# A fifth chunk of the second MLP matmul in rounded passes instead of fp32

## Chip, core and metric

The kernel runs on one core of a Trainium2 chip. The metric is the device time of one execution in microseconds (us), as the median of several runs. Engines are named as in the profile: PE is TensorE's matmul, PEld its weight load, DVE is VectorE, ACT is ScalarE, POOL is GpSimd, SP issues the transfers.

## What is computed

The input is x, 4 images of 128 channels and 112 x 112 points, fp32. Two blocks follow each other, each as x = x + block(groupnorm(x)). The first is window attention on 8 x 8 windows. The second is linear attention over the whole image with a depthwise convolution and an MLP; the change is in its MLP:

```python
out = out @ Wproj + bproj                                  # after the depthwise convolution
t = _repbn(t + out, bn1_g, bn1_b, bn1_m, bn1_v, alpha1)
ff = jax.nn.gelu(t @ Wfc1 + bfc1, approximate=False) @ Wfc2 + bfc2
t = _repbn(t + ff, bn2_g, bn2_b, bn2_m, bn2_v, alpha2)
```

Wfc1 is 128 x 1024, Wfc2 1024 x 128.

## The kernel before

One image after another goes through three stages, its x staying in SBUF (`ximg`): window attention, the statistics of the linear attention, and a stage over 28 blocks of 4 image rows (448 columns), which does the rest of the second block. The change is in this last stage, here called the MLP stage; it runs 28 steps per image, 112 in all. The program is written by hand, engine by engine, in a fixed order with semaphores, and the loop over blocks is unrolled four steps at a time (`block_loop`).

The hidden width of 1024 is cut in 8 chunks of 128, j = 0 to 7. In step B:

- PE (`step_d`, `fc1`, `fc2`) does the first matmul of chunk j into one of four PSUM banks, and from j = 4 on, behind it, the second matmul of chunk j - 4, added up in bank 6 or 7. Between them stand matmuls for other blocks: q of block B+4 after chunk 1, the projection of block B+1 after chunk 5, and the attention's output of block B+4 after chunk 7. Then come the second matmuls of chunks 4, 5, 6 and 7, and the next step's first matmul of chunk 0.
- ACT (`hidden`) takes each chunk out of PSUM with a GELU, and between chunks does evacuations and roundings for other blocks: qf and qh after chunk 1, tbh after chunk 2, t1h and wb after chunk 5, oring, ub and dwh around the end of the step.
- DVE does the nine taps of the depthwise convolution for block B+2, and around them subtractions (dwl, ql, tbl, t1l), a normalisation (tf), the mix t1 (the row t) after the projection, and the output yb.
- POOL subtracts hl and adds the residual xw for the next block.

A matmul comes in two forms. In fp32 one call gives two weight loads and two matmul records. In rounded form (`split_mm`, L1090 to L1092) both operands are split into a rounded part ("hi", type fp32r) and what is left over ("lo"), and three passes are added: hi x hi, lo weights x hi, hi weights x lo. All first matmuls and the matmuls for other blocks have the rounded form. Of the second matmul's chunks, those in `SPLIT_J`, 0, 2, 3 and 5, have it, and 1, 4, 6 and 7 are fp32.

A chunk in rounded form costs its operand two more operations. ACT writes the GELU to one of two buffers `hf` (L667) and copies it rounded to `hh` (L670); POOL subtracts the two into `hl` (L489), in the order of the chunks. A chunk in fp32 form has only the GELU, into `hw` (L661). Since `hf` has two buffers, the GELU of the k-th split chunk waits until POOL is done with split chunk k - 2. In the second matmul PE waits for `hl` of that chunk:

```python
k = SPLIT_J.index(j)                                       # ACT, hidden(B, j)
if k >= 2:
    act.wait_ge(hl_ready, B * NS + k - 1)
a.activation(hf[:, k % 2, :], bank[j % FC1_BANKS][:, 0:BLOCK], ACT.Gelu, ...)
act.wait_ge(hf_ready, H + 1)
a.activation(hh[:, k, :], hf[:, k % 2, :], ACT.Copy).then_inc(hh_ready, 1)

for k in range(NS):                                        # POOL, step_d
    pool.wait_ge(hh_ready, B * NS + k + 1)
    g.tensor_tensor(hl[:, k, :], hf[:, k % 2, :], hh[:, k, :].bitcast(F32), ALU.subtract)

pe.wait_ge(hl_ready, B * NS + k + 1)                       # PE, fc2(B, bb, j)
m = split_mm(out, [w[:, k, :] for w in w2s], [hh[:, k, :], hl[:, k, :]], ...)
```

At the start of the program ACT rounds the weights of the split chunks (L504) and DVE subtracts (L742).

Of the kernel before, what the change touches and what calls it, by code (L numbers as in the profile page):

```python
# [45 lines left out]
CM = 1024  # L46
NF = CM // P
QUADS_D = BLOCKS // 4
SPLIT_J = (0, 2, 3, 5)
NS = len(SPLIT_J)  # L50
WHOLE_J = tuple(j for j in range(NF) if j not in SPLIT_J)
FC1_BANKS = 4
# [16 lines left out]
def build(nc, x_d, vec_d, fc1b_d, dw_d, wm_d, cm_d, w1_d, w2_d, sel_d, out_d):  # L69
    with ExitStack() as ctx:  # L70
# [428 lines left out]
        def _(act):  # L499
            a = nc.scalar  # L500
            act.wait_ge(consts_loaded, 16 * NCONST)
            a.activation(w1s[0][:], w1f[:], ACT.Copy)
            for k, j in enumerate(SPLIT_J):
                a.activation(w2s[0][:, k, :], w2[:, j, :], ACT.Copy)  # L504
# [85 lines left out]
            with act.Fori(0, NIMG) as i:  # L590
# [64 lines left out]
                def hidden(B, j):  # L655
# [3 lines left out]
                    act.wait_ge(h_mm, H + 1)  # L659
                    if j not in SPLIT_J:  # L660
                        a.activation(hw[:, WHOLE_J.index(j), :], bank[j % FC1_BANKS][:, 0:BLOCK], ACT.Gelu,  # L661
                                     bias=fc1b[:, j:j + 1]).then_inc(hf_ready, 1)
                        return
                    k = SPLIT_J.index(j)
                    if k >= 2:
# [41 lines left out]
        def _(dve):  # L707
# [32 lines left out]
            d.tensor_tensor(w1s[1][:], w1f[:], w1s[0][:].bitcast(F32), ALU.subtract)  # L740
            for k, j in enumerate(SPLIT_J):
                d.tensor_tensor(w2s[1][:, k, :], w2[:, j, :], w2s[0][:, k, :].bitcast(F32), ALU.subtract)  # L742
# [667 lines left out]
```

## Time and profile before

| | us |
|---|---|
| median of 3 runs | 3083.43 (3077.89 to 3096.36) |
| the profiled execution | 3058.93 |
| its span, first to last instruction | 3057.1 |
| busy in it: PE | 2660.9 (87%) |
| PEld | 2194.2 (72%) |
| DVE | 2283.3 (75%) |
| ACT | 2133.7 (70%) |
| POOL | 1310.8 (43%) |

Durations below are from the profiled execution. A timeline row gives start, duration, engine, line, operation, output <- inputs, shapes, how many were merged (x2: two in a row, with the time from the first's start to the last's end), and in brackets the engine's idle time before it and what ended that. Records of PE overlap, since matmuls are pipelined: the distance from one weight load to the next tells what a pass costs.

### The profile page before, as it was taken

How to read it: one execution, taken by the hardware profiler on the slowest of the kernel's cores; microseconds unless marked ns; L12 is line 12 of the kernel's file. 1: busy time of each engine (PE TensorE's matmuls, PEld its weight loads, DVE VectorE, ACT ScalarE, POOL GpSimd, SP SyncE). 2: the span in 40 equal slices, each digit the busy share in tenths (PEclk: the TensorE clock that was granted, in tenths of full speed). 3: DMA queues.
4: the chain of work that ended last, by engine and by line, in shares of the span. 5: the costliest groups of instructions: out<-in, count | busy, mean ns of one | idle time of the engine just before them, and what ended most of it. 6: DMA issues, size and time to landing. Idle time of an engine off the chain costs nothing.

```text
span 3057.1 us, 76969 instructions
## 1 busy us (share of the span) xinstructions
PE 2660.9 (87%) x28146; PEld 2194.2 (72%) x28146; DVE 2283.3 (75%) x5017; ACT 2133.7 (70%) x4040; POOL 1310.8 (43%) x1210
## 2 busy tenths in 40 slices
PE   2888779999688877999958887799996888879999
PEld 2777678888477766888847777688875776768887
DVE  5777578888377757888747775788875777578885
ACT  2666458998466645998836664689984666468897
POOL 2444334555244432554524443345553444425454
PEclk9999889999799988999979998899997999889999
DMA  3000001111000000111100000011110000000000
GB/s 113 1 0 0 1 0 37 39 36 38 22 1 0 0 1 3 37 36 41 41 14 0 0 1 1 4 40 42 36 40 11 0 0 1 1 7 19 21 18 22
DMA packets 25541, 55.50 MB, mean 18 GB/s; under 512 B 3248, under 2 KB 17584, under 8 KB 25392
## 3 DMA queue, kind: packets, MB, share of 16 engines
q1 hardware_dynamic: 25392, 53.57, 5.3%
q8 instruction: 86, 1.41, 0.2%
q14 instruction: 63, 0.52, 0.1%
HBM read 27.87 MB, written 25.69 MB: 18 GB/s over the span
## 4 chain that ended last, share of the span: by engine, by line
PE 55%; issue 20%; POOL 9%; ACT 9%; DVE 4%; DMA 2%; POOLq 0%; SPq 0%; DVEq 0%; ACTq 0%
PE bank L1090 12%; PE bank L1092 11%; PE bank L1091 11%; PE bank L1307 10%; PE bank L1238 5%; POOL xn_lo L422 4%; POOL k L430 3%; PE bank L1246 3%; ACT kx L532 2%; ACT qs L523 2%; ACT kx L530 2%; DMA ximg<-x_in 1%; DVE bank L956 1%; PE bank L1143 1%; POOL hl L489 1%
## 5 line engine op out<-in xcount | busy, mean ns | idle before, releaser
L489 POOL TENSOR_TENSOR hl<-hf,hh 128x448 fp32r<-128x448 f32 x448 | 516.8, 1154 | 642.6 <-ACT hh L670 642.6
L956 DVE SCALAR_TENSOR_TENSOR bank<-oring,dw,bank 128x448 f32<-128x448 f32 x896 | 614.8, 686 | 20.8
L1307 PE MATMUL bank<-hw,w 128*128 128x448 f32 x896 | 390.8, 538 | 0.0
L1090 PE MATMUL bank<-t1h,w_hi 128*128 128x448 f32 x896 | 366.3, 409 | 24.1 <-DVE t1l L973 24.1
L667 ACT ACTIVATE hf<-bank,fc1b 128x448 f32<-128x448 f32 x448 | 282.1, 630 | 127.6 <-PE bank L1092 127.6
L422 POOL TENSOR_TENSOR xn_lo<-xn,xn_hi 128x512 fp32r<-128x512 f32 x112 | 127.2, 1136 | 481.9 <-ACT xn_hi L517 481.9
L1092 PE MATMUL bank<-t1l,w_hi 128*128 128x448 f32 x896 | 329.2, 367 | 0.0
L1091 PE MATMUL bank<-t1h,w_lo 128*128 128x448 f32 x896 | 327.9, 366 | 0.0
L807 DVE TENSOR_REDUCE mx<-bank 128x8 bf16<-128x512 f32 x448 | 248.3, 616 | 103.4 <-PE bank L1124 103.3
L523 ACT ACTIVATE qs<-bank,par 128x512 f32<-128x512 f32 x112 | 71.0, 634 | 329.6 <-PE bank L1092 329.6
L670 ACT ACTIVATE hh<-hf 128x448 fp32r<-128x448 f32 x448 | 259.3, 579 | 14.2
L661 ACT ACTIVATE hw<-bank,fc1b 128x448 f32<-128x448 f32 x448 | 266.4, 618 | 1.6 <-PE bank L1092 1.6
L1155 PE MATMUL bank<-vx,prob 128*64 128x34 f32 x6272 | 204.6, 225 | 46.2 <-ACT vx L538 44.2
L1155 PEld LDWEIGHTS bank<-vx,prob 128*64 128x64 f32 x6272 | 192.0, 138 | 63.1 <-ACT vx L538 52.6
L788 DVE TENSOR_SCALAR xc<-bank,lnmv,lnrs 128x128 f32<-128x128 f32 x392 | 135.2, 404 | 133.9 <-POOL lnrs L416 133.9
L476 POOL TENSOR_TENSOR xw<-wb,ximg 128x448 f32<-128x448 f32 x112 | 166.7, 1488 | 141.1 <-ACT wb L652 129.4
L1090 PEld LDWEIGHTS bank<-t1h,w_hi 128*128 128x128 f32 x896 | 169.7, 189 | 59.3 <-DVE t1l L973 26.5
L546 ACT ACTIVATE prob<-bank 128x512 f32<-128x512 f32 x448 | 205.9, 551 | 5.7 <-PE bank L1143 5.7
L1307 PEld LDWEIGHTS bank<-hw,w 128*128 128x128 f32 x896 | 168.2, 188 | 52.1 <-issue 41.9
L1090 PE MATMUL bank<-hh,w_hi 128*128 128x448 f32 x448 | 203.6, 454 | 2.3
L1143 PE MATMUL bank<-qs,kx 32*128 32x64 f32 x6272 | 197.2, 273 | 0.0
L1091 PEld LDWEIGHTS bank<-t1h,w_lo 128*128 128x128 f32 x896 | 169.5, 189 | 33.6 <-issue 20.8
(158 smaller groups left out, 6907.1 us busy)
## 6 DMA issues: line engine op xcount, KB each, us to landing
ximg<-x_in SPq DMA_DIRECT2D x56, 448.0 KB, 3.5
y_out<-yb SPq DMA_DIRECT2D x112, 224.0 KB, 1.9
wm<-wm_in SPq DMA_DIRECT2D x1, 512.0 KB, 3.4
w1f<-w_in SPq DMA_DIRECT2D x1, 512.0 KB, 5.6
w<-w_in SPq DMA_DIRECT2D x1, 512.0 KB, 6.5
cm<-cm_in SPq DMA_DIRECT2D x1, 320.0 KB, 3.7
sel_f<-sel_in SPq DMA_DIRECT2D x4, 64.0 KB, 6.2
vec<-vec_in SPq DMA_DIRECT2D x1, 11.0 KB, 1.6
```

The costliest lines, as they stand in the source:

```text
L422: g.tensor_tensor(xns[1][:, gg, 0:n], xn[:, gg, 0:n], xns[0][:, gg, 0:n].bitcast(F32), ALU.subtract).then_inc(xnl_ready, 1)
L489: g.tensor_tensor(hl[:, k, :], hf[:, k % 2, :], hh[:, k, :].bitcast(F32), ALU.subtract).then_inc(hl_ready, 1)
L661: a.activation(hw[:, WHOLE_J.index(j), :], bank[j % FC1_BANKS][:, 0:BLOCK], ACT.Gelu, bias=fc1b[:, j:j + 1]).then_inc(hf_ready, 1)
L667: a.activation(hf[:, k % 2, :], bank[j % FC1_BANKS][:, 0:BLOCK], ACT.Gelu, bias=fc1b[:, j:j + 1]).then_inc(hf_ready, 1)
L670: a.activation(hh[:, k, :], hf[:, k % 2, :], ACT.Copy).then_inc(hh_ready, 1)
L807: m = d.tensor_reduce(mx[:, gg, 32 * j:32 * j + 2 * n], bank[j][:, 0:P * n].rearrange("p (e k) -> p e k", k=64), AX.X, ALU.max)
L956: m = d.scalar_tensor_tensor(acc, src, dw[:, k:k + 1], acc, ALU.mult, ALU.add)
L1090: mm(out, w[0], x[0], start=start, stop=False)
L1091: mm(out, w[1], x[0], start=False, stop=False)
L1092: return mm(out, w[0], x[1], start=False, stop=stop)
L1155: m = mm(bank[6 + h][64 * w2:64 * w2 + 64, c:c + VCOLS], prob[:, j, 2 * t + w2, :], vx[:, gg, 2 * t + w2, j, :], start=True, stop=True)
L1307: m = mm(out, w2[:, j, :], hw[:, WHOLE_J.index(j), :], start=first, stop=last)
```

## The change

Chunk 4 joins the split chunks, so that five of the eight have the rounded form:

```diff
-SPLIT_J = (0, 2, 3, 5)
+SPLIT_J = (0, 2, 3, 4, 5)
 NS = len(SPLIT_J)
 WHOLE_J = tuple(j for j in range(NF) if j not in SPLIT_J)
```

All else follows from this tuple. `NS` is 5: `hh`, `hl` and the split second weights get a fifth slot, `hw` loses one, and the counts that engines wait for go by 5 per step. Chunks 4 and 5 are now k = 3 and k = 4, so the GELU of chunk 4 waits for `hl` of chunk 2, and that of chunk 5 for `hl` of chunk 3. POOL has five subtractions between two residuals xw in place of four. At the start there is one weight rounding more on ACT and one subtraction more on DVE.

On PE, at the end of a step, behind the attention's output (qh, ql with ctx):

```order
 L1091 MATMUL bank<-qh,ctx_lo 128x448
 L1092 MATMUL bank<-ql,ctx_hi 128x448
-L1306 REGISTER_ALU
-L1307 MATMUL bank<-hw,w 128x448
+L1302 REGISTER_ALU
+L1090 MATMUL bank<-hh,w_hi 128x448
+L1091 MATMUL bank<-hh,w_lo 128x448
+L1092 MATMUL bank<-hl,w_hi 128x448
 L1302 REGISTER_ALU
 L1090 MATMUL bank<-hh,w_hi 128x448
```

The fp32 matmul of chunk 4 went, and three passes stand in its place, right ahead of the three of chunk 5; the row ahead of each set (L1302) makes the count of `hl` that PE waits for.

On ACT, in the middle of a step, behind the rounding of chunk 3:

```order
 L670 ACTIVATE hh<-hf 128x448
 L659 REGISTER_ALU
-L661 ACTIVATE hw<-bank,fc1b 128x448
+L666 REGISTER_ALU
+L667 ACTIVATE hf<-bank,fc1b 128x448
+L670 ACTIVATE hh<-hf 128x448
 L659 REGISTER_ALU
 L666 REGISTER_ALU
```

The GELU of chunk 4 goes to `hf` instead of `hw`, with a wait for POOL ahead of it (L666) and the rounded copy behind it; chunk 5 follows.

## Rows read from the trace of the kernel before

**Rows 1.** MLP stage, first image, by stretch: busy us of PE, PEld, DVE, ACT, POOL; granted clock; DMA share, GB/s.
```profile
470.00:740.00 270.00, 270.00 (x1180) 221.19 (x1179) 234.67 (x375) 241.72 (x454) 137.39 (x114) 1.00 0.11 38
```

**Rows 2.** Timeline of PE's weight loads at the end of one step.
```profile
518.33 0.39 PEld L1307 LDWEIGHTS bank<-hw,w 128*128 128x128 f32 x2
...
520.26 0.19 PEld L1307 LDWEIGHTS bank<-hw,w 128*128 128x128 f32 x1 [0.19 <-issue]
520.64 0.19 PEld L1307 LDWEIGHTS bank<-hw,w 128*128 128x128 f32 x1 [0.19 <-issue]
...
521.39 0.19 PEld L1091 LDWEIGHTS bank<-t1h,w_lo 128*128 128x128 f32 x1 [0.19 <-issue]
521.60 0.19 PEld L1092 LDWEIGHTS bank<-t1l,w_hi 128*128 128x128 f32 x1
```

**Rows 3.** Timeline of ACT in the same step.
```profile
510.09 0.64 ACT L667 ACTIVATE hf<-bank,fc1b 128x448 f32<-128x448 f32 x1 [1.07 <-PE bank L1092]
...
515.55 0.62 ACT L661 ACTIVATE hw<-bank,fc1b 128x448 f32<-128x448 f32 x1
516.06 0.63 ACT L667 ACTIVATE hf<-bank,fc1b 128x448 f32<-128x448 f32 x1
516.72 0.58 ACT L670 ACTIVATE hh<-hf 128x448 fp32r<-128x448 f32 x1
517.21 0.56 ACT L651 ACTIVATE t1h<-t 128x448 fp32r<-128x448 f32 x1
...
522.20 0.64 ACT L667 ACTIVATE hf<-bank,fc1b 128x448 f32<-128x448 f32 x1 [1.09 <-PE bank L1092]
```

**Rows 4.** Timeline of POOL in the same step.
```profile
514.12 1.14 POOL L489 TENSOR_TENSOR hl<-hf,hh 128x448 fp32r<-128x448 f32 x1 [1.55 <-ACT hh L670]
515.72 1.16 POOL L489 TENSOR_TENSOR hl<-hf,hh 128x448 fp32r<-128x448 f32 x1 [0.46 <-ACT hh L670]
517.38 1.16 POOL L489 TENSOR_TENSOR hl<-hf,hh 128x448 fp32r<-128x448 f32 x1 [0.50 <-ACT hh L670]
518.70 1.52 POOL L476 TENSOR_TENSOR xw<-wb,ximg 128x448 f32<-128x448 f32 x1 [0.16 <-issue]
```

**Rows 5.** Timeline of DVE in the same step.
```profile
515.76 0.68 DVE L968 SCALAR_TENSOR_TENSOR t<-bank,par,ub 128x448 f32<-128x448 f32 x1 [0.69 <-PE bank L1092]
516.36 0.99 DVE L930 TENSOR_TENSOR tbl<-tf,tbh 128x448 fp32r<-128x448 f32 x1
...
518.59 0.62 DVE L973 TENSOR_TENSOR t1l<-t,t1h 128x448 fp32r<-128x448 f32 x1
```

**Rows 6.** The lines of tbl and of xw: duration in ns, min/median/max, all steps.
```profile
L930 DVE TENSOR_TENSOR tbl<-tf,tbh x112: 612/991/1011, 419.9 to 2991.8; 128x448 fp32r<-128x448 f32 x112
...
L476 POOL TENSOR_TENSOR xw<-wb,ximg x112: 1129/1522/1633, 444.6 to 3040.0; 128x448 f32<-128x448 f32 x112
```

**Rows 7.** Timeline of POOL late in the first image.
```profile
734.95 1.16 POOL L489 TENSOR_TENSOR hl<-hf,hh 128x448 fp32r<-128x448 f32 x1 [0.50 <-ACT hh L670]
736.17 1.42 POOL L476 TENSOR_TENSOR xw<-wb,ximg 128x448 f32<-128x448 f32 x1
```

**Rows 8.** Timeline of DVE late in the first image.
```profile
735.72 0.87 DVE L973 TENSOR_TENSOR t1l<-t,t1h 128x448 fp32r<-128x448 f32 x1
```

**Rows 9.** Timeline of PE's weight loads in one of an image's last four steps.
```profile
754.10 0.19 PEld L1090 LDWEIGHTS bank<-hh,w_hi 128*128 128x128 f32 x1 [0.52 <-POOL hl L489]
754.21 0.19 PEld L1091 LDWEIGHTS bank<-hh,w_lo 128*128 128x128 f32 x1
...
759.00 0.39 PEld L1307 LDWEIGHTS bank<-hw,w 128*128 128x128 f32 x2
```

**Rows 10.** Timeline of POOL in that step.
```profile
752.88 1.16 POOL L489 TENSOR_TENSOR hl<-hf,hh 128x448 fp32r<-128x448 f32 x1 [3.62 <-ACT hh L670]
754.54 2.28 POOL L489 TENSOR_TENSOR hl<-hf,hh 128x448 fp32r<-128x448 f32 x2 [0.50 <-ACT hh L670]
```

**Rows 11.** The line of the second weights' rounding on ACT: duration in ns, min/median/max.
```profile
L504 ACT ACTIVATE w_hi<-w x4: 292/292/293, 12.6 to 13.2; 128x128 fp32r<-128x128 f32 x4
```

## The prediction

> **What bounds the kernel now.** I read first the busy time by stretches, to find the stage that the change touches and the engine that fills it. In the MLP stage of the first image TensorE has 270.00 us busy of 270.00 and a granted clock of 1.00 (the 2.4 GHz level), while ACT has 241.72 and POOL 137.39 [rows 1]. Next I read one step of that stage, one 448-column block, from one engine's timeline to the next. ACT starts the GELU of chunk 0 at 510.09 and the same one of the next block at 522.20: a step takes 12.11 us [rows 3]. ACT stands idle 1.09 us before it, and the releaser is a TensorE matmul. So TensorE sets the pace; a step ends when its passes are through.
>
> What a chunk of the second matmul costs TensorE is read from the distance of the weight loads, since matmul records overlap. In the fp32 chunks 6 and 7 two loads stand 0.375 us apart (520.26, 520.64), and an fp32 chunk has two: 0.75 us. Rounded passes have loads 0.20 to 0.21 apart (521.39, 521.60): three passes, 0.61 us [rows 2].
>
> **The change, part by part.** One more chunk, j = 4, goes from one form to the other in all 112 steps.
>
> TensorE: per step one fp32 matmul goes (0.75) and three rounded ones come (0.61): 0.14 us less, 15.7 us in 112 steps, if its operands are there.
>
> ACT: the GELU of chunk 4 now writes hf and a rounding copy hh follows. A copy holds the queue 0.49 us (516.72 to 517.21), a GELU before its copy 0.66 (516.06 to 516.72) [rows 3], where the old GELU took 0.51 (515.55 to 516.06). So ACT carries 0.64 us more per step, and its 1.09 us of idle would hide that.
>
> POOL: a fifth subtraction hl per step, 1.14 to 1.16 us [rows 4]. POOL's total is far from full, but the five do not lie evenly: chunks 2 to 5 are now four subtractions in a row, and TensorE needs the last one soon. hf has only two buffers, so the GELU of chunk 5 must now also wait for the subtraction of chunk 3.
>
> So I follow one step in absolute time. Subtraction 2 ends at 514.12 + 1.14 = 515.26, ahead of GELU 4 at 515.55: no wait. The copy of 4 starts at 515.55 + 0.66 = 516.21 and ends 0.58 later, 516.79. Subtraction 3 ends at 515.72 + 1.16 = 516.88 [rows 4]. GELU 5 is released by that, about 516.94, its copy starts at 517.60 and ends at 518.18. On POOL, subtraction 4 could start at 516.88.
>
> Here VectorE comes in. Its subtraction tbl, also with two operands in SBUF, starts at 516.36 and lasts 0.99 us to 517.35 [rows 5], where its shortest is 0.612 and its median 0.991 [rows 6]: it gets going only when POOL is done at 516.88, and ends 0.47 later. Before the change nothing is ready on POOL just then: subtraction 5 starts at 517.38, when tbl is through. After it, subtraction 4 is at the door at 516.88, behind a VectorE instruction that already waits. The trace has this meeting once per image: t1l asks at 735.72 while POOL's subtraction runs (734.95 to 736.11), ends at 736.59, and POOL's next, xw, put down as starting at 736.17, ends only at 737.59 [rows 7, 8], 1.00 us after VectorE's end. In the ordinary step xw likewise ends at 520.22, 1.01 us after t1l's end at 519.21 [rows 4, 5]. So I price subtraction 4 at tbl's end plus 1.01 and 0.02 for hl being that much longer than xw where nothing holds it (1.129 at the least [rows 6], hl 1.14 to 1.16): 517.35 + 1.03 = 518.38. Subtraction 5 has its copy (518.18) and follows directly; two in a row take 2.28 us [rows 10], so 1.14 each: 519.52.
>
> The Trainium skill, SBUF — State Buffer, section "Who interferes with whom", says that a VectorE instruction with two SBUF inputs contends with a GpSimd instruction that reads SBUF, the second one blocking fully until the first is done. By that rule the sum is the one made here, +36.6 us; without it that of the first rival, +24. Rows 5 to 8 agree with it: tbl and t1l wait, and then POOL does.
>
> TensorE: how soon it goes on after POOL is seen at the end of an image, where it already waits for a subtraction. That ends at 752.88 + 1.16 = 754.04, and the second weight load, which marks the true start of the first pass, follows at 754.21 [rows 9, 10]: 0.17 us. Chunk 4's first pass starts at 518.33 + 0.20 = 518.53 before [rows 2]; subtraction 4 allows 518.55, a stall of 0.02. Chunk 5 is then due at 519.16, but allowed at 519.52 + 0.17 = 519.69: a stall of 0.53. Net per full step: 0.02 + 0.53 - 0.14 = +0.41 us, a step of 12.52. ACT's own delay does not decide: its copy of 5 ends 0.2 us before POOL comes free, and what follows it (t1h, wb, two GELUs, oring, ub, dwh) moves by 517.60 - 516.72 = 0.88 us, within the 1.09 + 0.41 that ACT then has. t1h now runs from 518.09 to 518.65 (it took 0.56 at 517.21 [rows 3]), so t1l finds subtraction 5 at work until 519.52 and ends near 520.0 in place of 519.21; VectorE is idle 35.3 of the 270 us of rows 1, 1.6 us a step, 0.69 of it before its mix [rows 5], so I take nothing for it. If that cover were gone, all 0.8 us would show.
>
> This holds for the 23 steps of an image in which tbl runs. The last five lack it, and the last four also lack q's two evacuations, so POOL's inputs come earlier. In one of the last four (its chunk 0 is subtracted from 752.88) subtractions 2 and 3 run from 754.54 to 756.82 [rows 10], so GELU 4 is released at 755.76, GELU 5 at 756.9, and the same reckoning gives subtraction 5 an end of 759.36, so 759.53 on TensorE, against 759.00 + 0.20 + 0.61 = 759.81 when chunk 5 is due [rows 9]: no stall, -0.14. I take that for four of the five. In the very last step the projection for a next block is missing, TensorE comes 0.61 earlier and stalls 0.33: +0.19. Per image 23 x 0.41 - 4 x 0.14 + 0.19 = 9.06; four images +36.2.
>
> Setup: one more rounding of a 128x128 weight on ACT, 0.29 us [rows 11], and one subtraction of the same size on VectorE, taken as equal; both lie ahead of TensorE's start, bounds 0 and 0.6, taken +0.4. The longer program costs nothing in my sum: the loop is already unrolled four times, and TensorE is full in it [rows 1].
>
> Sum: +36.6 us on the profiled execution of 3058.93, 3095.5, which is +1.2%. The median of the runs shown, 3083.43, is 0.8% above that execution; the same share gives 3083.4 + 36.9 = 3120.
>
> **The rivals.**
> VectorE and POOL do not hold each other up here. Then subtraction 4 runs 516.88 to 518.03, subtraction 5 starts when its copy is done (518.18 + 0.07) and ends 519.40; TensorE goes on at 519.57, a stall of 0.43, net +0.29 per full step, +24 us, 3107. For it: tbl might get through differently when POOL has work queued. Against it: rows 7 and 8.
>
> The gain stays. Subtraction 5 would have to be done by 519.14 - 0.17 = 518.97, 0.55 earlier than I reckon; ACT and POOL would have to drop behind less than their queues show. Then -15.7 us, 3068, not slower. For it: both engines have idle time in total [rows 1]. Against it: the old subtraction 5 ended at 517.38 + 1.16 = 518.54, only 0.6 us ahead of that point, and one more in front costs 1.1.
>
> A second meeting. If t1l is ready before subtraction 5 starts, VectorE takes its turn in between, 0.48 us more per full step: 92 x 0.48 = 44 on top, 3164. It decides from the point where subtraction 4 ends after 518.7, when t1h is done; I reckon 518.38, so it needs 0.3 us of further delay on POOL.
>
> **How the numbers follow.** Forecast 0.62, engines not holding each other up 0.20, gain stays 0.10, second meeting 0.08. A measurement of this kernel tells about 1% from no change. The forecast, +1.2%, lies just over that: about four fifths of its chance counts as slower (0.49), with the second meeting (0.08) and a little of the first rival (0.03) 0.60; the rest of the forecast (0.13), the first rival (0.17) and most of the gain (0.07) make 0.37 within 1%; 0.03 is left for faster. The range reaches down past the first rival, with the spread of the runs, to 3092, and up to 3150, between forecast and second meeting.
>
> **What would show it.** In the changed profile I expect: steps of about 12.5 us in place of 12.11; a wait of TensorE's weight load for hl of some 0.5 us once per full step, near nothing before; subtraction 4 with a record near 1.5 us; the wait of GELU 5 for POOL, 0.2 to 0.3 us; ACT's idle before GELU 0 at about 0.5. Steps near 11.97 and no wait for hl would make the prediction wrong, as would a subtraction 4 of 1.16 us beside a tbl of 0.99.

## The result and the profile after

| | before | after |
|---|---|---|
| median of 20 runs, us | 3075.82 (3060.12 to 3096.36) | 3098.98 (3089.57 to 3106.16) |
| ratio after / before | | 1.0071, 95% interval 1.0053 to 1.0089 |
| the profiled execution, us | 3058.93 | 3101.64 |
| MLP stage, first to last yb of an image, us | 323.3 in all four | 330.7 in all four |
| a full step of it, us | 12.11 | 12.47 |

The ratio is an estimate with its interval; the quotient of the two medians is 1.0075. The kernel became slower, by less than forecast: 3098.98 us where 3120 was said, +0.7% where +1.2% was said. A second comparison, with the same two kernels (e8 below), gave 1.0087 (1.0063 to 1.0111).

The stage first. TensorE, full before [rows 1], is idle 5 of 270 us; ACT and POOL have more to do; the granted clock is 1.00 again. Since records of PE overlap, this idle time shows only part of what TensorE loses, 0.23 us a step where the passes come 0.50 late, as the weight loads below tell.

```profile
470.00:740.00 270.00, 264.81 (x1170) 215.92 (x1169) 244.20 (x365) 249.63 (x465) 162.13 (x130) 1.00 0.11 38
```

What TensorE waits for is in the view of the waits of the same stretch (total us, times, longest). The second and the last row shown stand in no such view of the kernel before: in 22 steps the first weight load of a split chunk waits 0.6 us for hl, and its matmul up to 0.2.

```profile
ACT hf L667 <- PE bank L1092: 14.1, 22, 0.7
PEld bank L1090 <- POOL hl L489: 13.4, 22, 0.6
...
PE bank L1090 <- POOL hl L489: 5.2, 22, 0.2
```

One full step, engine by engine. ACT (answers to [rows 3]): GELU 0 at 524.86 and 537.34, 12.48 us apart; the copy of chunk 4 at 530.97; then GELU 5 does not follow 0.49 later, at 531.46, but at 531.68, when subtraction 3 is done:

```profile
524.86 0.63 ACT L667 ACTIVATE hf<-bank,fc1b 128x448 f32<-128x448 f32 x1 [0.70 <-PE bank L1092]
...
530.97 0.58 ACT L670 ACTIVATE hh<-hf 128x448 fp32r<-128x448 f32 x1
531.68 0.64 ACT L667 ACTIVATE hf<-bank,fc1b 128x448 f32<-128x448 f32 x1
532.35 0.58 ACT L670 ACTIVATE hh<-hf 128x448 fp32r<-128x448 f32 x1
...
537.34 0.63 ACT L667 ACTIVATE hf<-bank,fc1b 128x448 f32<-128x448 f32 x1 [0.69 <-PE bank L1092]
```

POOL (answers to [rows 4]): subtractions 3, 4 and 5 now run without a gap and are merged in one row. They take 3.77 us, where three at 1.155 would take 3.46: the middle one is stretched to about 1.46.

```profile
528.89 1.15 POOL L489 TENSOR_TENSOR hl<-hf,hh 128x448 fp32r<-128x448 f32 x1 [1.55 <-ACT hh L670]
530.49 3.77 POOL L489 TENSOR_TENSOR hl<-hf,hh 128x448 fp32r<-128x448 f32 x3 [0.45 <-ACT hh L670]
534.33 1.42 POOL L476 TENSOR_TENSOR xw<-wb,ximg 128x448 f32<-128x448 f32 x1
```

VectorE (answers to [rows 5]): tbl waits for subtraction 3 and ends at 532.12, and t1l, 0.62 us before, now takes 1.31, since it meets subtraction 5:

```profile
531.14 0.98 DVE L930 TENSOR_TENSOR tbl<-tf,tbh 128x448 fp32r<-128x448 f32 x1
...
533.43 1.31 DVE L973 TENSOR_TENSOR t1l<-t,t1h 128x448 fp32r<-128x448 f32 x1
```

TensorE's weight loads (answers to [rows 2]): chunk 4's second load is at 533.31; chunk 5's would be due 0.61 later at 533.92 and is at 534.42, 0.16 behind POOL's end at 534.26:

```profile
533.20 0.19 PEld L1090 LDWEIGHTS bank<-hh,w_hi 128*128 128x128 f32 x1
533.31 0.19 PEld L1091 LDWEIGHTS bank<-hh,w_lo 128*128 128x128 f32 x1
533.51 0.19 PEld L1092 LDWEIGHTS bank<-hl,w_hi 128*128 128x128 f32 x1
534.31 0.19 PEld L1090 LDWEIGHTS bank<-hh,w_hi 128*128 128x128 f32 x1 [0.61 <-POOL hl L489]
534.42 0.19 PEld L1091 LDWEIGHTS bank<-hh,w_lo 128*128 128x128 f32 x1
```

### The profile page after: what moved, and what is told of

Same layout as the page of the kernel before. It is cut to its first block, busy times and chain, and to the rows that moved or that the text cites. A ratio compares the mean times of both kernels' runs of the same rounds, so it can differ in the third digit from the quotient of the medians.

```text
span 3099.8 us, 77643 instructions
## 1 busy us (share of the span) xinstructions
PE 2692.7 (87%) x28258; PEld 2219.9 (72%) x28258; DVE 2355.4 (76%) x5018; ACT 2204.0 (71%) x4153; POOL 1457.6 (47%) x1322
## 4 chain that ended last, share of the span: by engine, by line
issue 36%; POOL 32%; PE 17%; ACT 8%; DVE 4%; DMA 2%; POOLq 1%; SPq 0%; DVEq 0%; ACTq 0%
POOL hl L489 20%; PE bank L1238 5%; POOL xw L476 4%; POOL xn_lo L422 4%; POOL k L430 3%; PE bank L1090 3%; PE bank L1246 3%; ACT kx L532 2%; ACT kx L530 2%; ACT qs L523 2%; PE bank L1092 2%; PE bank L1091 2%; DMA ximg<-x_in 1%; PE bank L1143 1%; DVE bank L956 1%
## 5 line engine op out<-in xcount | busy, mean ns | idle before, releaser
L489 POOL TENSOR_TENSOR hl<-hf,hh 128x448 fp32r<-128x448 f32 x560 | 672.4, 1212 | 542.8 <-ACT hh L670 542.8
L667 ACT ACTIVATE hf<-bank,fc1b 128x448 f32<-128x448 f32 x560 | 351.9, 628 | 94.9 <-PE bank L1092 79.8
L670 ACT ACTIVATE hh<-hf 128x448 fp32r<-128x448 f32 x560 | 324.3, 579 | 17.8
L1307 PE MATMUL bank<-hw,w 128*128 128x448 f32 x672 | 288.6, 538 | 0.0
L1090 PE MATMUL bank<-hh,w_hi 128*128 128x448 f32 x560 | 216.4, 386 | 22.9 <-POOL hl L489 20.7
L476 POOL TENSOR_TENSOR xw<-wb,ximg 128x448 f32<-128x448 f32 x112 | 160.2, 1431 | 126.3 <-ACT wb L652 121.2
L1091 PE MATMUL bank<-hh,w_lo 128*128 128x448 f32 x560 | 205.0, 366 | 0.0
L1092 PE MATMUL bank<-hl,w_hi 128*128 128x448 f32 x560 | 202.9, 362 | 0.0
L661 ACT ACTIVATE hw<-bank,fc1b 128x448 f32<-128x448 f32 x336 | 196.5, 617 | 0.0
```

The source lines that it names most:

```text
L476: g.tensor_tensor(xw[:, bb, :], wb[:, bb, :], ximg[:, bass.ds(b * BLOCK, BLOCK)], ALU.add).then_inc(xw_ready, 1)
L1090: mm(out, w[0], x[0], start=start, stop=False)
L1091: mm(out, w[1], x[0], start=False, stop=False)
L1092: return mm(out, w[0], x[1], start=False, stop=stop)
L1307: m = mm(out, w2[:, j, :], hw[:, WHOLE_J.index(j), :], start=first, stop=last)
```

## The experiments

Steps and stages below are worked out from the starts of yb (L982): a stage is the first to the last yb of an image, a full step the mean from the third to the 23rd. Each execution comes with its mean granted clock, so kernels can also be compared at equal clock: a straight line with one slope for all kernels through the 124 executions with a recorded clock gives 1.8 us for each 0.001 and leaves 1.9 us of scatter. In the last column the kernel before itself differs by 2.0 us between the executions beside e1 to e4 (3070.1) and those beside e5 to e8 (3072.0), so differences of that size say nothing there.

| | change | full step | MLP stage | ratio to before (95%) | at a clock of 0.950 |
|---|---|---|---|---|---|
| before | | 12.11 | 323.3 | | 3071.0 (54 runs) |
| after | | 12.47 | 330.7 | 1.0071 (1.0053 to 1.0089) | 3098.6 (20) |
| e1 | before, unaltered | 12.11 | 323.2 | 0.9996 (0.9975 to 1.0018) | in the first row |
| e2 | after, tbl late | 12.39 | 328.8 | 1.0072 (1.0047 to 1.0097) | 3088.4 (4) |
| e3 | after, third hf | 12.49 | 330.8 | 1.0092 (1.0066 to 1.0119) | 3098.6 (4) |
| e4 | after, both | 12.13 | 322.9 | 0.9950 (0.9928 to 0.9972) | 3063.8 (6) |
| e5 | after, late wait for hl | 12.18 | 322.7 | 0.9965 (0.9947 to 0.9984) | 3066.3 (12) |
| e6 | after, all three | 11.97 | 317.7 | 0.9929 (0.9904 to 0.9953) | 3045.7 (6) |
| e7 | before, late wait for hl | 12.11 | 321.6 | 0.9981 (0.9961 to 1.0002) | 3063.5 (12) |
| e8 | after, unaltered | 12.48 | 330.9 | 1.0087 (1.0063 to 1.0111) | 3099.9 (6) |

**e1, the kernel before once more.** No edit.

> The kernel before, unaltered, to see how its own executions spread and what clock each had. Theory of the clock: the executions differ outside the MLP stage, in window attention, by the granted clock; the times of this kernel fall along one line against the clock (about 1.4 us for each 0.001, read from the 20 executions of the changed kernel), and at a clock of 0.956 they lie near 3059, some 30 us under the changed kernel at the same clock; the median lies near 3076 because the usual clock is lower than the 0.956 of the profiled execution. MLP stage from the first to the last yb of an image: 323.3 us in every image, granted clock 1.00. Rival: TensorE, full in the MLP stage, is slowed there in most executions, and the changed kernel hides part of that in its stalls; then the profile shows MLP stages over 324 us or a granted clock under 1.00 in them.

Measured: MLP stages of 323.2 in all four images, where the first trace has 323.3; the rival (TensorE slowed there) falls. The executions of the kernel before, this one's and those beside it, run from 3065.76 us at a clock of 0.953 to 3090.61 at 0.939. So the profiled execution of 3058.93 at 0.956 that the prediction started from was one of the quickest, and what spreads the runs lies outside the MLP stage. By the line above they follow the clock at 1.8 us for each 0.001, not 1.4. The window attention of single images in the two first traces, from its first xg (L766) to its last, shows it. The kernel before, third image, 265 us at a clock of 0.96:

```profile
1560.27:1825.44 265.17, 223.71 (x4402) 180.98 (x4406) 199.71 (x624) 167.43 (x321) 110.95 (x126) 0.96 0.00 0
```

and the kernel after, third and fourth image, 0.92 for 273 us and 0.97 for 265, with the same number of PE's instructions:

```profile
1577.48:1850.15 272.67, 233.53 (x4402) 189.35 (x4406) 199.76 (x624) 167.29 (x321) 110.67 (x126) 0.92 0.00 0
2349.94:2614.95 265.01, 223.14 (x4402) 180.58 (x4406) 199.85 (x624) 167.20 (x321) 110.67 (x126) 0.97 0.00 0
```

Each is a mixture of the two levels, 1.2 and 2.4 GHz (0.50 and 1.00), and the low one lies at its beginning: in the kernel before the first 24 us have 0.58 and the rest 1.00, in the kernel after the first 40 us have 0.56:

```profile
1560.00:1584.00 24.00, 12.88 (x119) 9.83 (x123) 11.12 (x41) 7.66 (x14) 7.24 (x10) 0.58 0.00 1
1584.00:1825.00 241.00, 210.39 (x4286) 170.96 (x4283) 188.15 (x581) 159.76 (x308) 103.60 (x117) 1.00 0.00 0
```

```profile
1577.00:1617.00 40.00, 28.83 (x327) 23.94 (x328) 20.02 (x68) 13.59 (x24) 11.61 (x15) 0.56 0.00 1
```

The statistics stage varies likewise, in e1 from 150.5 us at 0.86 to 156.7 at 0.80. Long and short ones stand in traces of both kernels: in e1, the kernel before, window attention takes 264.7 us in one image and 273.4 in another. Of the 42.7 us between the two profiled executions, 16.8 are of this kind (window attention and statistics of all four images, from the first xg to the first yb: 1683.6 us against 1666.8).

**e2, tbl at the end of the step.**

```diff
-                    if near(5):
-                        tb_low(B + 5, (u + 1) % 2)
                     if near(2):
                         taps(B + 2, (u + 2) % 4, 5, 7, not near(3))
...
                         taps(B + 2, (u + 2) % 4, 7, NTAP, not near(3))
+                    if near(5):
+                        tb_low(B + 5, (u + 1) % 2)
```

> The changed kernel with VectorE's tbl moved from the middle of the step to its end, away from POOL's four subtractions. Theory A (POOL's queue, with the turn that tbl takes in it): subtraction 4 has a record of 1.15 us and ends 0.35 us earlier, but subtraction 5 then waits for its copy (the GELU of chunk 5 still waits for subtraction 3), so it ends only 0.10 earlier, 9.30 us after GELU 0 in place of 9.40: a step of 12.38 us in place of 12.48, MLP stage 328.5 per image in place of 330.7, 9 us less in all. Rival B (tbl and POOL do not hold each other up): no change, 12.48. Rival C (the fp32 matmul's going is not worth 0.14 and the stall is not POOL's): no change.

Measured: 12.39 and 328.8. Subtractions 3 and 4 take 2.29 us together, no longer stretched, and subtraction 5 starts only 0.24 us after them, for want of its copy:

```profile
530.45 1.15 POOL L489 TENSOR_TENSOR hl<-hf,hh 128x448 fp32r<-128x448 f32 x1 [1.55 <-ACT hh L670]
532.05 2.29 POOL L489 TENSOR_TENSOR hl<-hf,hh 128x448 fp32r<-128x448 f32 x2 [0.45 <-ACT hh L670]
534.57 1.15 POOL L489 TENSOR_TENSOR hl<-hf,hh 128x448 fp32r<-128x448 f32 x1 [0.24 <-ACT hh L670]
```

So the turn that tbl takes is real, and what it costs alone is 0.09 us a step, because the copy of chunk 5 is right behind as the next limit. The plain ratio did not move; its four runs had a mean clock of 0.9455. At equal clock it is 10 us below the kernel after, where 7.8 were due from the stages.

**e3, a third hf buffer.**

```diff
-        hf = sb("hf", [P, 2, BLOCK])
+        hf = sb("hf", [P, 3, BLOCK])
...
-                    if k >= 2:
-                        act.wait_ge(hl_ready, B * NS + k - 1)
-                    a.activation(hf[:, k % 2, :], ...)
+                    if k >= 3:
+                        act.wait_ge(hl_ready, B * NS + k - 2)
+                    a.activation(hf[:, k % 3, :], ...)
```

The copy and POOL's subtraction take the same slot, k % 3.

> The changed kernel with a third hf buffer, so that the GELU of chunk 5 waits for subtraction 2 instead of 3. Theory A: the wait of that GELU for POOL (0.23 us) goes, but subtraction 5 still stands behind subtraction 4 in POOL's queue; step 12.48 us, MLP stage 330.7 per image, no change within 1 us. Rival D (the two hf buffers are what delays chunk 5): 0.25 us less per full step, 12.23, some 23 us less in all.

Measured: 12.49 and 330.8, no change; subtractions 3 to 5 take the same 3.77 us:

```profile
528.15 3.77 POOL L489 TENSOR_TENSOR hl<-hf,hh 128x448 fp32r<-128x448 f32 x3 [0.46 <-ACT hh L670]
```

Rival D falls: ACT's wait for the buffer does not decide here. That it is a second limit, 0.2 us below the first, shows in the next run.

**e4, both.** The edits of e2 and e3 together.

> The changed kernel with both: tbl at the end of the step and a third hf buffer. Theory A: subtraction 4 ends at 7.92 us after GELU 0 and subtraction 5, its copy done at 7.84, at 9.07; TensorE's stall falls from 0.53 to 0.2 us; step 12.15 us in place of 12.48, MLP stage near 323 per image, 30 us less in all, which is the kernel before within 0.2%. Rival D: no more than the third buffer alone gives, 12.23. Rival B: what the third buffer alone gives.

Measured: 12.13 and 322.9. The three subtractions take 3.42 us, and TensorE's wait falls from 0.6 to 0.3:

```profile
533.42 3.42 POOL L489 TENSOR_TENSOR hl<-hf,hh 128x448 fp32r<-128x448 f32 x3 [0.45 <-ACT hh L670]
```

```profile
PEld bank L1090 <- POOL hl L489: 6.0, 22, 0.3
```

Neither edit alone was worth more than 0.09 us a step, both are worth 0.34. That is what two limits in a row look like, the POOL queue and, 0.1 to 0.2 us below it, the copy.

**e5, the wait for hl ahead of the third pass only.**

```diff
-                        pe.wait_ge(hl_ready, B * NS + k + 1)
-                        m = split_mm(out, [w[:, k, :] for w in w2s], [hh[:, k, :], hl[:, k, :]],
-                                     start=first, stop=last)
+                        pe.wait_ge(hh_ready, B * NS + k + 1)
+                        mm(out, w2s[0][:, k, :], hh[:, k, :], start=first, stop=False)
+                        mm(out, w2s[1][:, k, :], hh[:, k, :], start=False, stop=False)
+                        pe.wait_ge(hl_ready, B * NS + k + 1)
+                        m = mm(out, w2s[0][:, k, :], hl[:, k, :], start=False, stop=last)
```

> The changed kernel, but TensorE waits for the subtraction hl only ahead of the third pass of a split chunk, the one that reads it; the first two passes wait for the copy hh. Theory A (TensorE's stall is for subtraction 5, whose copy is long done): the third pass of chunk 5 is due 0.41 us after the first, so the stall of 0.53 us per full step falls to about 0.1; step 12.08 us in place of 12.48. In the last four steps of an image the stall of 0.42 at chunk 0, which the kernel before has too, also goes. MLP stage near 320.5 us per image (330.7 changed, 323.3 before). Against the kernel before at equal clock some 11 us less. Rival D (ACT's late copy of chunk 5 is what TensorE waits for): the stall stays, 12.4.

Measured: 12.18 and 322.7, so 0.29 of the 0.40 us came back; 0.10 a step did not. The waits of the weight loads name two causes, hl at the third pass and, new, ACT's GELU of chunk 6, which comes behind the later GELU 5 and the added copy (L1309 is the fp32 matmul, L1306 the third pass):

```profile
PEld bank L1309 <- ACT hw L661: 4.9, 22, 0.2
PEld bank L1306 <- POOL hl L489: 4.8, 22, 0.2
```

A weight load can wait 0.2 us without a loss: e6 below, where TensorE is full, has a row like the first of these. What each costs TensorE shows in the matmul records of one step beside those of e6. The third pass of chunk 5 takes 0.47 us in place of 0.36, and the four fp32 records of chunks 6 and 7 take 1.77 in place of 1.67, about 0.1 us each. The latter in e5 and in e6:

```profile
534.18 1.77 PE L1309 MATMUL bank<-hw,w 128*128 128x448 f32 x4
```

```profile
519.32 1.67 PE L1309 MATMUL bank<-hw,w 128*128 128x448 f32 x4
```

Theory A stands for the stall, about 0.1 us as said, but not for what is next: I had taken ACT's idle time as cover and had not worked out when GELU 6 is due once TensorE comes earlier. Rival D falls: chunk 5's first pass now follows without a wait.

**e6, all three.** The edits of e2, e3 and e5.

> All three: tbl at the end of the step, a third hf buffer, and the wait for hl ahead of the third pass alone. Theory A: subtraction 5 ends 9.07 us after GELU 0 and the third pass is due at 9.46, so no stall is left and the whole 0.14 us of the fifth chunk shows: step 11.97 us, MLP stage near 317.8 per image, against the kernel before some 22 us less at equal clock (0.7% faster), of which 6 to 7 come from the stall at chunk 0 in the last four steps of an image. Rival (another engine, ACT or VectorE, takes over once TensorE no longer waits for POOL): step 12.05 or more.

Measured: 11.97 and 317.7, and 0.9929 of the kernel before: faster than both. TensorE is full again, and the rival falls:

```profile
470.00:740.00 270.00, 270.00 (x1219) 227.68 (x1219) 248.29 (x380) 256.58 (x484) 159.35 (x137) 1.00 0.12 39
```

The weight loads of the third passes of chunks 4 and 5 stand 0.60 us apart, without a wait for POOL:

```profile
518.31 0.19 PEld L1306 LDWEIGHTS bank<-hl,w_hi 128*128 128x128 f32 x1
...
518.91 0.19 PEld L1306 LDWEIGHTS bank<-hl,w_hi 128*128 128x128 f32 x1
```

**e7, the kernel before with the late wait.** The edit of e5 on the kernel before.

> The kernel before with the wait for hl ahead of the third pass alone, to tell how much of the run with all three is not the fifth chunk's. Theory A: full steps stay at 12.11 us, since nothing stalls there; the last four steps of an image lose 0.42 us each: MLP stage 321.6 per image in place of 323.3, 6.7 us less in all. Rival: the late wait itself shortens full steps: under 12.05.

Measured: full steps 12.11, stage 321.6, as said. It parts the gain of e6: the stages of e6 are 317.72 - 321.63 = -3.91 us per image against this one, -15.6 in four (27 of 28 steps in each), which is the 15.7 that the change promised on TensorE (112 x 0.14).

**e8, the kernel after once more.** No edit.

> The changed kernel, unaltered, once more beside the kernel before on this chip. Theory of the clock: MLP stage 330.7 per image again, and at equal clock some 29 us above the kernel before; the plain ratio may differ from that by what the mean clocks differ (0.0039 higher here in the first comparison, worth 7 us). If the clock difference was chance, the plain ratio is 1.009 to 1.010; if it belongs to the kernel, 1.007 again.

Measured: stage 330.9, ratio 1.0087, between the two expectations, with an interval that holds 1.007 as well as 1.010. The medians lie 29.7 us apart here, 23.2 in the first comparison. The mean clock was 0.9485 here and 0.9495 for the kernel before beside it, so here the kernel after had the lower one; in the first comparison it had 0.950, but for the kernel before beside it none is on record. At equal clock the kernel after lies 27.6 us (the 20 executions of the first comparison) and 28.9 us (the six here) above the 54 of the kernel before, 0.9%.

## Why the prediction was right and wrong

The direction and the mechanism were right, the size was not.

- That TensorE fills the stage and that an fp32 chunk costs it 0.75 us and a rounded one 0.61: right. e6 against e7 shows the difference, 15.6 us of 15.7.
- That the fifth subtraction reaches TensorE too late: right. Subtraction 5 was put at 9.43 us after GELU 0 and came at 9.40 (534.26 - 524.86); the stall was put at 0.53 and is 0.50.
- That tbl takes a turn between subtractions 3 and 4: right. The second of three is stretched to 1.46 us, and e2 removes that. The first rival, without the turn, falls. By e2 the turn is worth 0.09 us a step, where the forecast and this rival lie 0.12 apart.
- That ACT's own delay does not decide: right by e3, though by little, as e4 shows. That it is covered was right only as long as TensorE stalls; e5 shows GELU 6 as the next wait. ACT's idle before GELU 0 is 0.69 us, where about 0.5 was expected.
- t1l's delay at no cost: the step lengths agree. Its end came at 534.74, 9.88 after GELU 0, where 9.9 was said.
- The second meeting (t1l between subtractions 4 and 5) did not happen: t1l asked at 533.43, subtraction 5 had begun by then.

The step that failed is the sum, "+36.6 us on the profiled execution": the full step and what lies between the images were mis-sized, and the time of 3120 stood on too high a base.

- The full step, "+0.41 us": measured +0.36. I priced subtraction 4 at tbl's end plus 1.03 and it was about 1.00 (534.26 less 1.14, less 532.12); so chunk 4 does not stall at all, where 0.02 was said, and the rest is rounding over five durations. Also, the first of the 23 steps, which lies ahead of the first yb, hardly stalls: its weight load waits 0.25 us in place of 0.61. In the last five steps the sum held: four become 0.15 to 0.17 us shorter (from one GELU 0 to the next) where 0.14 was said, the last 0.16 longer (from yb to yb) where 0.19 was said. From the first to the last yb this makes 7.46 us per image where the sum has 9.06: 29.8 in place of 36.2.
- What lies between the images, taken as unchanged: from the last yb to the next image's first xg (L766) it took 17.9, 18.5 and 13.4 us before and 16.5, 16.7 and 12.6 after, 4.0 us less in all. SP waits there for the last store before it loads the last strip of the next image; in the first image the load is issued 3.78 us after that store before the change, and 2.12 after it. Before:

```profile
785.22 0.34 SPq L357 DMA_DIRECT2D y_out<-yb  x1
789.00 0.37 SPq L372 DMA_DIRECT2D ximg<-x_in  x1
```

After:

```profile
793.53 0.34 SPq L357 DMA_DIRECT2D y_out<-yb  x1
795.65 0.36 SPq L372 DMA_DIRECT2D ximg<-x_in  x1
```

This does not come every time. In the traces of all runs the load follows the store by 3.4 us or more in 8 of 9 such places with four split chunks (before, e1, e7), but also in 2 of 21 with five (e3, e8); in the others by 2.1 to 2.4. Why the store lands sooner was not traced.

- The time of 3120 was put on the median of three runs, 3083.43; the median of twenty is 3075.82.
- The clock outside the MLP stage, also taken as unchanged. The plain medians of the first comparison lie 23.2 us apart, some 5 less than the 28 at equal clock; that would fit a mean clock some 0.003 higher in the changed kernel's runs, but for the 20 runs of before in that comparison no clock is on record, and in e8 the difference was the other way. So this share is argued, not shown.

Together: of the 21 us between 3120 and 3099, 7.6 are the base, 6.4 the MLP stage, about 4 what lies between the images, and some 3 are left to the clock and the scatter. At equal clock, stage and ends give 26 us of the 28 measured; the rest was not traced.

The first rival's sum has a slip: 92 x 0.29 with the same last steps and setup makes +25.6 us, 3109, not +24 and 3107. That the medians of the first comparison, 23.2 apart, lie nearer to it than to the forecast is chance: its mechanism is refuted, and the step itself, +0.36, lies between its +0.29 and the forecast's +0.41.

Of the chances: with a sum of +1.2% beside a bound of 1%, an error of 0.2% in the sum was enough to turn the likeliest case. I had the scatter of the runs before my eyes and gave 0.60 to "slower by over 1%"; terms read to 0.02 us a step, times 92, already make 2 us.

## What to carry to other kernels

Moving work off the bounding engine is worth its price only if the operands come in time: follow the last operand through the queue that makes it, and count what stands ahead of it there, not the engine's idle total. When a wait is found, look for the second limit right under it (here 0.1 to 0.2 us lower): removing one alone gave at most 0.09 us a step, both together 0.34 of the 0.36 lost. Where one pass of several reads the late operand, put the wait ahead of that pass.

## What the runs showed of the hardware

- A VectorE subtraction with two SBUF operands that waits for a running POOL subtraction goes ahead of POOL's next one: three POOL subtractions in a row take 3.77 us with tbl in the middle and 3.42 without (e3, e4). Taken away alone it was worth 0.09 us a step (e2).
- The same program, the kernel before, differs by up to 37 us from execution to execution (3059 to 3096), with the MLP stage at 323.2 to 323.3 in both traces of it; the time follows the mean granted clock at 1.8 us for each 0.001, and the low stretches lie in window attention and the statistics. What sets them was not tried.
